# Selective stage's first turns with scores ahead of films, and the spectra's products spread over ten turns of the ternary stage

## The reference, cut to what matters

```python
def _L2_ffn_ref(x, ternary_weight, bias, act_scale):
    scale = jnp.maximum(act_scale, 1e-05)
    x_int = jnp.clip(jnp.round(x / scale), -QB, QB)
    ...
    w = ternary_weight.astype(jnp.float32) - 1.0
    return jnp.einsum('bsi,oi->bso', x_dq, w) + bias

def _L3_xattn_ref(x_text, x_vision, text_mask, vision_mask, Wq, Wk, Wv, W_film_in, ...):
    def s4d(x, log_dt, A_re, A_im, C_re, C_im, D_skip):
        ...
        powers = jnp.exp(dtA[:, :, None] * jnp.arange(L))
        K = 2.0 * jnp.einsum('dn,dnl->dl', dC, powers).real
        Kf = jnp.fft.rfft(K, n=n, axis=-1)
        xf = jnp.fft.rfft(x, n=n, axis=1)
        y = jnp.fft.irfft(xf * Kf.T[None], n=n, axis=1)[:, :L]
        return y + x * D_skip
    ...
    topv, topi = jax.lax.top_k(scores, K_TOP)            # 32 of 120, four heads
    probs = jax.nn.softmax(topv, axis=-1)
    attn_mean = attn.mean(axis=1)
    c_t = jnp.einsum('btg,bgd->btd', attn_mean, V)
    x = layernorm(x_text, g_norm_in, b_norm_in)
    scale_in, shift_in = jnp.split(c_t @ W_film_in + b_film_in, 2, axis=-1)
    x = x * (1.0 + mod_gate * scale_in) + mod_gate * shift_in
    y = s4d(x, log_dt, A_re, A_im, C_re, C_im, D_skip)
    scale_out, shift_out = jnp.split(c_t @ W_film_out + b_film_out, 2, axis=-1)
    y = y * (1.0 + mod_gate * scale_out) + mod_gate * shift_out
    xt = x_text + y
    h = layernorm(xt, g_ffn, b_ffn)
    h = jax.nn.gelu(h @ W1 + b1, approximate=False) @ W2 + b2
    return layernorm(xt + h, g_norm_out, b_norm_out)
```

## Time and profile before

| | |
|---|---|
| runs, us | 4198.76, 4198.76, 4194.62 (median 4198.76) |
| profiled execution, us | 4196.49 |
| its span, first to last instruction, us | 4194.7 |
| mean granted clock of TensorE | 0.972 of 2.4 GHz |
| PE busy | 3932.5 us, 94% |
| DVE busy | 3195.8 us, 76% |
| ACT busy | 2286.0 us, 54% |
| POOL busy | 655.4 us, 16% |
| ternary stage, from PE's first operation to DVE's last | 3255.92 to 3327.64 |
| first operations of the selective stage | 3327.92 |

### The profile page before, as it was taken

How to read it: one execution, slowest core, us unless ns; L and a number is a source line. 1 busy time by engine, 2 the same in 40 slices (tenths; PEclk the granted TensorE clock), 3 DMA queues, 4 the chain that set the end, 5 groups by cost and what they waited for, 6 DMA issues and landing times. The chain is left out here.

```text
span 4194.7 us, 69443 instructions
## 1 busy us (share of the span) xinstructions
PE 3932.5 (94%) x22744; PEld 3103.0 (74%) x22744; DVE 3195.8 (76%) x7648; ACT 2286.0 (54%) x5428; POOL 655.4 (16%) x1193
## 2 busy tenths in 40 slices
PE   8997999999799999999999999999999679999788
PEld 6886777777587887887878878788787456667566
DVE  7996777888577777777777777777777689999457
ACT  4445665555566565665656655556565134444344
POOL 3432331111500000000000000000033423333201
PEclk9999999999799999999999999999999689999899
DMA  4001000000000000000000000000000200000101
GB/s 105 0 0 46 6 7 3 0 0 0 20 3 2 4 1 3 4 2 5 1 2 5 2 5 1 2 5 2 2 1 11 70 1 1 0 0 0 43 1 41
DMA packets 37504, 42.87 MB, mean 10 GB/s; under 512 B 7020, under 2 KB 33712, under 8 KB 37176
## 3 DMA queue, kind: packets, MB, share of 16 engines
q1 hardware_dynamic: 36440, 39.25, 3.4%
q10 hardware_dynamic: 800, 0.33, 0.0%
HBM read 35.11 MB, written 4.19 MB: 9 GB/s over the span
## 5 line engine op out<-in xcount | busy, mean ns | idle before, releaser
L1843 ACT ACTIVATE global_prob_t_high<-psum 128x512 fp32r<-128x512 f32 x960 | 570.3, 601 | 560.6 <-PE psum L1954 560.6
L1752 DVE TENSOR_TENSOR global_prob_t_low<-psum,global_prob_t_high 128x512 fp32r<-128x512 f32 x960 | 657.0, 690 | 248.1 <-ACT global_prob_t_high L1843 239.2
L1758 DVE TENSOR_REDUCE global_top<-psum 128x1 f32<-128x480 f32 x1024 | 666.5, 657 | 116.6 <-PE psum L1914 111.7
L1912 PE MATMUL psum<-global_prob_t_high,global_v_low 128*128 128x512 f32 x960 | 455.6, 475 | 1.1
L1912 PE MATMUL psum<-global_k_high,global_q_low 128*128 128x480 f32 x1024 | 391.2, 382 | 15.9 <-ACT spare L1864 13.8
L1914 PE MATMUL psum<-global_k_high,global_q_high 128*128 128x480 f32 x1024 | 391.9, 383 | 0.0
L1913 PE MATMUL psum<-global_k_low,global_q_high 128*128 128x480 f32 x1024 | 389.4, 380 | 0.0
L1913 PE MATMUL psum<-global_prob_t_low,global_v_high 128*128 128x512 f32 x960 | 379.5, 395 | 0.0
L1914 PE MATMUL psum<-global_prob_t_high,global_v_high 128*128 128x512 f32 x960 | 379.0, 395 | 0.0
L1864 ACT ACTIVATE spare<-psum,global_bias 128x480 f32<-128x480 f32 x512 | 337.6, 663 | 18.4 <-DVE global_bias L1761 17.0
L1864 ACT ACTIVATE global_prob<-psum,global_bias 128x480 f32<-128x480 f32 x512 | 337.7, 663 | 1.2
(11 more groups left out here) (473 smaller groups left out, 8190.5 us busy)
## 6 DMA issues: line engine op xcount, KB each, us to landing
x_res<-in_x SPq DMA_DIRECT2D x8, 512.0 KB, 14.6
moe_we<-in_expert_t SPq DMA_DIRECT2D x8, 512.0 KB
out<-x_res SPq DMA_DIRECT2D x16, 256.0 KB, 2.1
cho_wqkv<-in_L_ffn_Wqkv SPq DMA_DIRECT2D x2, 1536.0 KB, 10.0
moe_last_row<-in_expert_t SPq DMA_DIRECT2D x16, 128.0 KB, 3.1
sel_w<-in_L_xattn_W SPq DMA_DIRECT2D x2, 1024.0 KB, 11.2
self_ctx_t<-in_ctx_t SPq DMA_DIRECT2D x1, 1440.0 KB, 12.2
global_ctx_t<-in_ctx_t SPq DMA_DIRECT2D x1, 1440.0 KB, 8.9
```

What stands on the lines that cost most here:

```text
L1752: dve.tensor_tensor(dst, psum, high.bitcast(F32), ALU.subtract).then_inc(ready.sem, 1)
L1758: ins = dve.tensor_reduce(top[:, c:c + 1], w.psum[:, c, 0:chunk], AX.X, ALU.max)
L1843: act.activation(dst, psum, ACT.Copy).then_inc(ready.sem, 1)
L1912: pe.matmul(to, lhs_low, rhs_high, start=start, stop=False)
```

## The change

**Ternary stage.** `spectrum` now makes one product, a step; the 20 steps are laid two a turn into turns 6 to 15, in the order of before. The wait for the gathered lags stands in turn 6. ACT's copies move to turns 10 and 14, and the last one behind all turns.

**Selective stage.** The five turns ahead of the loop become seven: the block at F no longer shares a turn with T in them. The order is M0; M1 T0; M2 T1; F0 alone; M3 T2 now0; F1 alone; then the full turn M4 T3 F2 now1 done0 as before. PE waits in a lone F turn also for DVE to have taken the scores of the next block. `prepare_rows` moves behind the first statistics, `prepare_bias` behind block 0's u, `shift_b1` behind the scores of block 1, POOL's first context copy to the head of its function, and the wait for `w1_ready` from ahead of `forward` of block 0 to ahead of its `backward`.

```diff
+    SPECTRA_FROM, STEPS_A_TURN = 6, 2
...
-                if t == 11:
+                if t == SPECTRA_FROM + 4:
                     act.wait_ge(spectrum_psum.sem, spectrum_psum.count(0))
...
-                if t == 12:
+                if t == SPECTRA_FROM + 8:
                     act.wait_ge(spectrum_psum.sem, spectrum_psum.count(1))
...
-                if t == 13:
-                    act.wait_ge(spectrum_psum.sem, spectrum_psum.count(2))
-                    act.activation(by_last[:, 0, :], spectrum_at[4], ACT.Copy)
+            act.wait_ge(spectrum_psum.sem, spectrum_psum.count(2))
+            act.activation(by_last[:, 0, :], spectrum_at[4], ACT.Copy)
...
-            def spectrum(part):
-                for b in range(B_STEPS):
-                    last = pe.matmul(spectrum_at[part], transform[:, b, part * P:(part + 1) * P],
-                                     lags[:, :, :, b].rearrange("a e g -> a g e"),
-                                     start=(b == 0), stop=(b == B_STEPS - 1))
-                return last
+            def spectrum(step):
+                part, b = step // B_STEPS, step % B_STEPS
+                last = pe.matmul(spectrum_at[part], transform[:, b, part * P:(part + 1) * P],
+                                 lags[:, :, :, b].rearrange("a e g -> a g e"),
+                                 start=(b == 0), stop=(b == B_STEPS - 1))
+                if b == B_STEPS - 1 and part in (1, 3, 4):
+                    last.then_inc(spectrum_psum.sem, 1)
...
-                if t == 10:
+                if t == SPECTRA_FROM:
                     pe.wait_ge(transform_loaded.sem, 16)
                     pe.wait_ge(gathered.sem, 16 * GROUP * B_PARTS)
...
+                if t >= SPECTRA_FROM:
+                    for n in range(STEPS_A_TURN):
+                        spectrum((t - SPECTRA_FROM) * STEPS_A_TURN + n)
...
-        for n in range(-3, 2):
-            iteration((n + 3, (n + 3) % 2), (n + 2, n % 2) if n >= -2 else None, (n + 1, (n + 1) % 2) if n >= -1 else None,
-                      (n, n % 2) if n >= 0 else None, n - 1 if n >= 1 else None)
+        iteration((0, 0), None, None, None, None)
+        iteration((1, 1), (0, 0), None, None, None)
+        iteration((2, 0), (1, 1), None, None, None)
+        iteration(None, None, (0, 0), None, None)
+        iteration((3, 1), (2, 0), None, (0, 0), None)
+        iteration(None, None, (1, 1), None, None)
+        iteration((4, 0), (3, 1), (2, 0), (1, 1), 0)
...
+            pool.tensor_copy(ctx_b[:, :, :], ctx_t[:, :, 0, :]).then_inc(sig("ctx_copied").sem, 1)
             chain.link(pool.memset(minus_one[:, :], -1.0))
...
                     stats("a", i, x_tile(i))
+                    if isinstance(i, int) and i == 0:
+                        prepare_rows()
...
                                       ALU.add).then_inc(sig("u_base").sem, 1)
+                    if isinstance(i, int) and i == 0:
+                        prepare_bias()
...
                     need(pe, "mean_ready", i)
+                    if T is None and isinstance(i, int) and i < 2:
+                        need(pe, "scores_kept", i + 1)
```

21 lines of the change are left out of this document (5 added, 16 removed).

## The result

| | before | after |
|---|---|---|
| median of 11 runs, us | 4198.76 | 4208.02 |
| lowest to highest, us | 4194.62 to 4203.86 | 4204.16 to 4212.41 |
| profiled execution, us | 4196.49 | 4209.01 |
| its span, us | 4194.7 | 4207.2 |

The ratio is 1.0022, with a 95% interval of 1.0014 to 1.003: the change costs 9.3 us at the median. The interval leaves out 1, so the kernel is slower, by little more than the least that such runs can tell from none. One run of the kernel before, beside the four experiments from "one lone film" to "shift behind films", took 11509.48 us, and the medians there leave it out.

A forecast was written before the change was run, and what follows sets the result against it. PE was taken as busy for most of the span with DVE next to it, DVE binding the ternary stage until 3302. Ternary +3.7 and selective +4.1 (-5.5 + 8.4 + 1.2) make 7.8 us, forecast 4204.8 us, range 4196 to 4210.

The forecast's parts named there:

- Rival (b): Selective stage: clock low through both film chains and forward 1, giving 4209 to 4210 us; chance 0.2.
- The gate: Ternary stage: PE waits some 10.6 us in turn 6 for the gathered lags; the stage ends 3.7 us later.
- rival (a): Ternary stage: the clock rises in the mixed work, ternary part 0, about 4201.5 us; chance 0.16.
- Rival (d): Ternary stage: the gather does not gate, the stage ends 7.3 us earlier, 4193.5 us; chance 0.04.
- The head: Start of the selective stage: statistics first, preparations in DVE's waits, 4.8 us gained until DVE's first masked scores.
- Second scores: Selective stage, block 1's scores ahead of the films: 5.1 us more gained, at 36.7 us from the stage's start.
- F0: Turn 0's product with `forward`: 5.5 us earlier against the selective stage's start, bounds 10.2 and 2.2 earlier.
- The second chain: Between forward 0 and forward 1: block 1's lone films put in series, 8.4 us lost.
- The clock: Between forward 0 and forward 1: PE's idling lowers the clock, half the price of one `forward`, 1.2 us lost.
- (c): Selective stage: the lead survives, block-1 chain at 2.4 GHz, ternary +3.7, selective -2, 4198 us; chance 0.1.
- Rival (e): Ternary stage: spectra not spread but start as a block of waiting at the gate; part of the forecast, same time.

The follow-up runs named there:

- one lone film: The two-queue kernel with block 1's films put back into the turn with T = 2 and now = 0: 4187.42 us, ratio 0.9979.
- shift behind films: The kernel with the rows later, with `shift_b1` moved from behind block 1's scores to behind film out of block 0: 4181.17 us, ratio 0.9963.
- two-queue kernel: The changed kernel with the gather split over SP (18 DMAs) and ACT (14), spectra two a turn from turn 7: 4197.24 us, ratio 0.9998.
- the kernel of the table's last row: The changed kernel with block 1's films put back into the turn with T = 2 and now = 0: 4199.69 us, ratio 1.0002.
- the four kernels with both lone turns: The changed kernel, its selective part alone, it with spectra four a turn from turn 10, and the two-queue kernel: 4208.02, 4202.12, 4201.83, 4197.24 us.
- the two joined ones: Block 1's films put back into the turn with T = 2, on the two-queue kernel (4187.42 us) and on the changed kernel (4199.69 us).
- the kernel with the rows later: One lone film with `prepare_rows` behind the second block's statistics and `prepare_bias` behind `scale_w1`: 4187.16 us, ratio 0.9973.
- the ternary part alone: The kernel before with only the ternary half of the change: 4201.60 us against 4198.47, ratio 1.0011.

## Why the prediction was right, and where it was not

The median, 4208.02, lies in the range (4196 to 4210), 3.2 us over the predicted 4204.8. The sum was 7.8 us; from T0 to F2 the trace has 10.8. "Within 0.2%" had the chance of 0.71, and the ratio of 1.0022 stands at that border, with most of its interval on the slower side; 0.25 for slower was too little. Rival (b) named the time best, 4209 to 4210. Its mechanism was true in part: the first film chain was at the low level, the second was not (film groups of 1.98 us), and F1 was for the larger part (5.21 us).

**The gate: right.** Predicted: the products start at 3300 to 3301 behind a wait of 10 to 11 us. Measured: 3300.82 behind 10.28, and with T0's shift of 0.9 taken off, 3299.9 for the forecast 3300.2. The clock did not leave 0.50, as the row said against rival (a). From the gate to the end of ACT's last copy the sum had 31.1 us; it took 31.8. Four records between two groups took 2.06 us (3304.23 to 3306.29), not the 1.9 that a fourth of a burst of 16 gives, and the turns 3.45 to 3.51 with one of 3.63. Stage +4.1 for +3.7, in the bounds. The two-queue kernel shows the cause: with the issues shared, the gate is gone and 8.9 us with it. Rival (d) gave 7.3 us under before to a stage without the gate; that kernel's is 4.8 under (67.1 for 71.9), with its spectra one turn later and turns of 3.45 us.

**The head: gain over-sized.** -4.8 forecast, -3.0 measured. The failing step is "`prepare_rows` and `prepare_bias` now lie in DVE's waits ...: nothing on the path". DVE did wait there, but POOL worked, and it was POOL that the path went through; with `prepare_rows` moved behind POOL's work the head took the forecast 11.0 us. The Trainium skill, "SBUF — State Buffer", section "SBUF: two separate sides", says of the pair of ports that the two engines share, for DVE operations in a mode with two ports and some with two inputs in SBUF, that it is an exclusive lock and "the other fully blocks". POOL's 1.20 us, ending with DVE's operation, agrees; in which mode that operation ran no trace shows.

**Second scores: 39.7 for 36.7.** 1.8 of the 3.0 is the head. Most of the rest is PE's clock and ACT behind it: PE's 16 records of `values_by_film` (L2804) took 10.12 us for 8.69 before, ACT's copies and then its exponentials came later, and DVE waited 2.41 us for them in place of 1.04. The sum had no term for this. With the same code up to there the kernel of the table's last row had 8.50 us and 38.0; the four kernels with both lone turns lie at 39.1 to 39.7, the two joined ones at 38.0 and 38.3. Why the clock rose later in the four is left open.

**F0: -1.9 for -5.5, outside its bounds of -10.2 to -2.2.** From the end of block 1's scores the sum had 27.8 us to F0; it took 29.0 (S + 39.0 to S + 68.0). The size was near, and in part by luck. The sum stood between the two clock levels; the trace has nearly all of the chain at the lower one, which by the sum's own prices makes 31. Cheaper than its rows were the contexts (6.0 us, where the sum had 4 and 2.8 more for 1.2 GHz) and the way from film out over ACT and POOL to k (7.0 us with film out at 1.2 GHz, where the sum had 6.1 at 2.4 GHz and 1.8 more for 1.2 GHz). What put F0 outside was the start, 2.4 us late from the two steps ahead. The bounds took in the clock but not the terms before them.

**The second chain: right in kind, 1.3 too large.** 8.4 forecast; measured 10.3 us between feed-forward and F1 for 1.85, less 1.4 that turn 0's body is shorter, makes 7.1. Film out to k took 5.2 us (3439.48 to 3444.66), not 6.1, and k with the transposes 0.8, not 1.2. The body's 1.4 for the forecast 1.3 is luck: the two film groups that left saved 3.1 us and F0 0.9 (5.31 for 6.21), while PE waited 1.3 more for ACT ahead of h's transposes and lost 1.5 in the contexts and the feed-forward at a lower clock. DVE's wait was 5.81 us, in the forecast 5 to 9. The joined kernels confirm the step: without the lone turn F2 follows F0 by 10.0 and 10.3 us less.

**The clock: under-sized, and in part at another place.** 1.2 us were set between F0 and F1, as half the price of one `forward` at the lower level. Against before, F0 gave 0.9 back, the body of turn 0 lost 1.5, and F1 itself, which lies behind its own mark, took 5.21 us for 3.69: 2.1 in all up to F2. From F1 to F2 it is 1.5 (36.7 for 35.2), and that is why +5.2 at F1 became +6.7 at F2.

**Together:** 0.4 from the ternary stage and 2.6 from the selective one are the 3.0 by which the sum fell short of the trace; the medians say 3.2 above the forecast, counted from the nearest value. The misses partly cancelled: F0 came 3.6 us later than forecast and 1.5 were lost behind F1, but between F0 and F1 the sum had 2.5 too much (9.6 for 7.1). That the total came so near is in part luck. The rows of the gate exclude rivals (a) and (d), and F0 excludes (c). Rival (e) was true as said: the spectra start as a block of waiting.

## What to carry to other kernels

Work that is laid into idle time brings its waits along: on an engine that takes its instructions in order, an operation put earlier must have its data earlier, so look at the landing time first, and at how many issues one queue has to make. When two blocks' steps are pulled apart at the filling of a pipeline, price every step that then stands alone in the chain, one-time work included; with `shift_b1` in front of the films a lead of 5 us in the second scores was worth nothing, and with it behind them, by the difference of two kernels, some 3. Idle time on one engine does not hide work if a second engine, on the path, shares something with it.

## What the runs showed of the hardware

- Small POOL operations (128x2) of 0.20 and 0.70 us took 1.20 and 1.49 beside DVE's wide operations on SBUF, and DVE's six operations of 1.86 us (block 1's mean) took 3.95 in the changed kernel beside two of POOL's of 1.26, 3.84 in the kernel with the rows later; where `scale_w1` stood beside them instead, its two operations together took 3.51 and 3.46 for 1.41 (one lone film, on two queues and on the changed kernel). Each engine slows the other, and an edit that moves either of them by some us shifts the loss to another place.
- A DMA of 8 KB from SBUF to SBUF cost its issuing queue about 0.63 us on SP (32 in 20.18) and 0.61 on ACT (4 in 2.45); two queues side by side each kept that rate.
- 29 us of PE without a pause, a mix of fp32 and bf16 products, stayed at the granted clock of 0.50 in three kernels (the changed one, the ternary part alone, two queues), while in the selective stage, 32.5 of 35 us busy, it was 1.00. What separates the two is left open here.
- T0 varied by 8.2 us over the thirteen traces with the same code ahead of it. To tell parts of a few us apart, a trace has to be read from a mark next to them.
